# Attention and a ternary feed-forward on one core: VectorE takes y's rounding constant off while it clips, the ones are written by other memsets, and all five orders are new

## The chip, the cores and the metric

One NeuronCore of a Trainium2 chip runs the whole program. Its five engines (TensorE, VectorE, ScalarE, GpSimd, SyncE) follow instruction streams of their own and meet only at semaphores. The metric is the device time of one launch in microseconds. A profile calls the engines PE (PEld for weight loads), DVE, ACT, POOL and SP.

## The reference

32 batches of 128 channels by 512 positions (f32). Each batch goes through

```
x = x + attention(layernorm(x), ctx)     8 heads of 16 channels, rope on 8 of the 16,
                                         softmax over the 512 keys
x = x + ffn(layernorm(x))                gate, up: 512 -> 2048; silu(gate) * up;
                                         Hadamard transform over 2048; down: 2048 -> 512
act_quant(x):    q = 128 / max(max|x|, 1e-5);  clip(round(x q), -128, 127) / q
weight_quant(w): s = 1 / max(mean|w|, 1e-5);   clip(round(w s), -1, 1) / s
```

Every product with a weight of the feed-forward takes act_quant of its input (the down product that of the transformed y) and weight_quant of the weight.

## The kernel before, in words

One batch fills the 128 partitions. Its attention works in head chunks: 32 `score_max` products of 128 x 512 (L439), whose row maxima VectorE takes (`reduce_scores`, L1009); the maxima are transposed and laid by DMA into one more row of the stacked q, against a row of ones in the stacked k; 32 `scores` products (L469) then come out with the maximum taken off, ScalarE puts each through the exponential (`exps`, L712), and eight `weigh` groups (L484) multiply by v. `score_max` n may start when `reduce_scores` n - 2 is done, and `scores` n when `exps` n - 2 is done, since each has two PSUM banks.

The feed-forward of the batch before runs in the gaps: `gate_up` products (L525), `half_gates` (L1095), a tanh (L736), `glu` (L1104) and `gate_product` on GpSimd (L1274); then GpSimd makes four butterfly stages of the Hadamard transform: three on each half of 1024 columns (`hadamard_half`, L1265 the sums and L1266 the differences, with a semaphore wait after each stage), and the last over both (`hadamard_last`, L1263). TensorE multiplies by the 128 x 128 Hadamard matrix (`hadamard`, L536), ScalarE copies the four results into `ys` (`y_out`, L764), VectorE finds the largest value and the factor (`quantise`, L1116 to L1120).

Each half j of y (128 x 1024) is then quantised in three steps: ScalarE multiplies and adds the constant 12582912, which rounds (`round_y`, L743, f32); ScalarE takes the constant off again and writes bf16 (`whole_y`, L753); VectorE takes the minimum with 127 in place, bf16 to bf16 (`clip_y`, L1128). `y_transpose` j (L547) waits for that, `yT_out` (L771) copies it, and `down` (L560) multiplies.

The order of each engine is written out by hand in a function `step(t)`, called for t from `FIRST` to `LAST`; each call names the batch it serves (t, t - 1 and so on) and does nothing where that batch doesn't exist. All engines execute in this order. The three weights are loaded, their absolute means found (`abs_piece`), rounded (`round_piece`) and reduced to signs (`sign_piece`) in pieces between the work of the first three batches; the SP queue issues all activation DMAs in the order of its own `step`. GpSimd writes the row of ones of the first two stacks of k before its loop (L1233, one partition) and fills the third stack (L1240, all partitions) in the loop. `rstd1` (L1247) is the root of the first norm.

Of the kernel before, what the change touches and what calls it, by code (L numbers as in the profile page):

```python
# [39 lines left out]
FIRST, LAST = -3, B + 5  # L40


def live(b):
    return 0 <= b < B
# [45 lines left out]
def layer(nc, x, ctx_in, proj_t, table_t, late_t, wg_t, wu_t, wd_t, out):  # L90
    stack = ExitStack()
    with stack:
# [119 lines left out]
        ones_set, ones_rows_set, third_ones_set = sem("ones_set"), sem("ones_rows_set"), sem("third_ones_set")  # L212
# [15 lines left out]
        factor_done, rounded, whole = sem("factor_done"), sem("rounded"), sem("whole")  # L228
# [53 lines left out]
        def _(sp):  # L282
# [16 lines left out]
            def stack_part(b, part):  # L299
# [73 lines left out]
        def _(pe):  # L373
# [81 lines left out]
            def scores(b, n):  # L455
# [6 lines left out]
                if n == 0 and b == 0:  # L462
                    pe.wait_ge(ones_rows_set, 2)
                if n == 0 and b == 2:
                    pe.wait_ge(third_ones_set, 1)
# [98 lines left out]
            def step(t):  # L564
                gate_up(t - 3, "up", 3)
                scores(t - 2, 16)
                scores(t - 2, 17)
                score_max(t - 1, 16)
                score_max(t - 1, 17)
                weigh(t - 2, 3)  # L570
                scores(t - 2, 18)
                score_max(t - 1, 18)
                score_max(t - 1, 19)
                scores(t - 2, 19)
                scores(t - 2, 20)
                score_max(t - 1, 20)
                scores(t - 2, 21)
                down(t - 4, 0, 4)
                score_max(t - 1, 21)
                scores(t - 2, 22)  # L580
                scores(t - 2, 23)
                score_max(t - 1, 22)
                weigh(t - 2, 4)
                scores(t - 2, 24)
                scores(t - 2, 25)
                score_max(t - 1, 23)
                weigh(t - 2, 5)
                scores(t - 2, 26)
                score_max(t - 1, 24)
                scores(t - 2, 27)  # L590
                score_max(t - 1, 25)
                scores(t - 2, 28)
                score_max(t - 1, 26)
                scores(t - 2, 29)
                y_transpose(t - 4, 1)
                scores(t - 2, 30)
                score_max(t - 1, 27)
                score_max(t - 1, 28)
# [791 lines left out]
```

## Time and profile before

| | |
|---|---|
| three runs | 1533.31 us median, 1532.55 to 1535.38 |
| the profiled execution | 1531.52 us |
| its span, first to last instruction | 1529.7 us, mean granted clock of TensorE 0.974 |
| busy of the span | PE 93%, DVE 86%, ACT 71%, POOL 72%, PEld 49% |
| DMA | 71 GB/s mean |

The span falls into a start of some 170 us, in which weights and first batches are set up, 28 steady frames, one per batch, and an end of some 90 us in which the last feed-forwards run out. In a table of a stretch the five busy times are those of PE, PEld, DVE, ACT and POOL, in this order. A row of a timeline gives the start in us from the beginning of the span, the duration, engine, line, operation, destination and source. Neighbouring instructions overlap by some 0.08 us in it, so what one instruction costs an engine is the distance of two starts.

### The profile page before, as it was taken

To read this page: it belongs to the slowest core of one execution; us is meant where nothing else is said; L and a number is where in the kernel's file an instruction comes from. 1 tells how busy PE (TensorE), PEld (TensorE's weight loads), DVE (VectorE), ACT (ScalarE), POOL (GpSimd) and SP (SyncE) were. 2 spreads that over 40 slices of the span, in tenths; PEclk is the share of its full clock that TensorE was granted. 3 is DMA by queue.
4 is the path that set the end of the run, shared out by engine and by line. 5 is a ranking of instruction groups with operands and counts; after the bars stand their busy time and mean duration, and the time that the engine had idled before them with its cause. 6 is when DMAs were issued, how large, how long until landed. Compare 5 with 4: busy or idle time off the path is not lost.

```text
span 1529.7 us, 30990 instructions
## 1 busy us (share of the span) xinstructions
PE 1424.7 (93%) x11042; PEld 743.8 (49%) x11042; DVE 1322.4 (86%) x2331; ACT 1082.5 (71%) x1777; POOL 1098.7 (72%) x812
## 2 busy tenths in 40 slices
PE   1688999999999999999999999999999999999983
PEld 1215455545555555455555544555555444555442
DVE  2768899999999999999999999999999999998641
ACT  3586677778777777787777777877777777777762
POOL 4124777887777778877777788777777887777674
PEclk9688999999999999999999999999999999999996
DMA  8861434434234344343244443332434443323000
GB/s 211 223 124 37 66 63 77 70 63 69 61 60 77 63 77 76 58 70 63 58 76 63 77 77 61 66 65 61 70 64 77 77 68 59 69 46 47 15 8 14
DMA packets 81112, 108.12 MB, mean 71 GB/s; under 512 B 9664, under 2 KB 59200, under 8 KB 79936
## 3 DMA queue, kind: packets, MB, share of 16 engines
q1 hardware_dynamic: 77744, 93.56, 35.4%
q10 hardware_dynamic: 3216, 12.58, 2.3%
q8 instruction: 89, 1.46, 0.4%
q14 instruction: 63, 0.52, 0.1%
HBM read 38.73 MB, written 8.39 MB: 31 GB/s over the span
## 4 chain that ended last, share of the span: by engine, by line
PE 71%; ACT 12%; DVE 5%; issue 4%; POOL 4%; DMA 2%; SPq 0%; POOLq 0%; ACTq 0%; DVEq 0%
PE s L469 12%; PE ring L525 12%; PE pv L484 12%; PE s L439 11%; PE ring L560 7%; PE ring L536 6%; ACT region L712 4%; PE ring L413 3%; PE ring L493 2%; ACT parts L779 2%; PE ring L547 2%; PE ring L427 2%; ACT y_last L753 1%; ACT y_last L771 1%; DVE maxima L1009 1%
## 5 line engine op out<-in xcount | busy, mean ns | idle before, releaser
L1009 DVE TENSOR_REDUCE maxima<-s 128x1 bf16<-128x512 f32 x1024 | 668.3, 682 | 60.1 <-PE s L439 55.6
L712 ACT ACTIVATE region<-s 128x512 f32<-128x512 f32 x1024 | 576.0, 597 | 133.3 <-PE s L469 123.8
L439 PE MATMUL s<-region 96*128 96x512 bf16 x1024 | 374.3, 391 | 21.7 <-DVE maxima L1009 11.5
L1274 POOL TENSOR_TENSOR region<-region,th 128x512 f32<-128x512 f32 x128 | 161.8, 1273 | 297.1 <-DVE th L1104 295.3
L469 PE MATMUL s<-region 97*128 97x512 bf16 x1024 | 362.2, 384 | 10.0 <-ACT region L712 4.8
L1265 POOL TENSOR_TENSOR region<-region 128x512 f32<-128x512 f32 x192 | 260.3, 1356 | 12.8
L484 PE MATMUL pv<-region,v_ext 128*17 128x512 f32 x2048 | 264.1, 599 | 0.0
L1266 POOL TENSOR_TENSOR region<-region 128x512 f32<-128x512 f32 x192 | 243.9, 1270 | 0.0
L439 PEld LDWEIGHTS s<-region 96*128 96x128 bf16 x1024 | 99.8, 98 | 198.6 <-DVE maxima L1009 74.2
L469 PEld LDWEIGHTS s<-region 97*128 97x128 bf16 x1024 | 93.2, 98 | 187.7 <-ACT region L712 154.1
L1263 POOL TENSOR_TENSOR region<-region 128x1024 f32<-128x1024 f32 x64 | 149.4, 2355 | 0.1
L794 ACT ACTIVATE v_ext<-ring 128x512 f32<-128x512 f32 x32 | 19.1, 598 | 180.7 <-PE ring L427 178.2
L536 PE MATMUL ring<-late_const,region 128*128 128x128 f32 x1024 | 132.7, 279 | 13.7 <-POOL region L1263 11.7
L525 PEld LDWEIGHTS ring<-xqT,wg 128*128 128x128 bf16 x2048 | 123.5, 98 | 42.5 <-issue 16.7
L525 PEld LDWEIGHTS ring<-xqT,wu 128*128 128x128 bf16 x2048 | 122.4, 98 | 44.7 <-issue 26.6
L525 PE MATMUL ring<-xqT,wg 128*128 128x128 bf16 x2048 | 136.0, 219 | 7.4 <-ACT xqT L721 6.9
L536 PEld LDWEIGHTS ring<-late_const,region 128*128 128x128 f32 x1024 | 129.0, 195 | 18.0 <-issue 13.6
L525 PE MATMUL ring<-xqT,wu 128*128 128x128 bf16 x2048 | 135.7, 219 | 2.2 <-ACT y_last L771 1.2
L560 PE MATMUL ring<-wd,y_last 128*128 128x512 bf16 x512 | 127.6, 382 | 1.6 <-ACT y_last L771 1.6
L1095 DVE TENSOR_TENSOR region<-ring,half_gate 128x512 f32<-128x512 f32 x128 | 87.5, 684 | 13.5 <-PE ring L525 9.5
L1308 POOL TENSOR_TENSOR region<-region,rope_c 64x1024 f32<-64x1024 f32 x32 | 75.6, 2362 | 31.5 <-DVE region L998 17.4
L1104 DVE SCALAR_TENSOR_TENSOR th<-th,ring 128x512 f32<-128x512 f32 x128 | 87.3, 682 | 5.5 <-PE ring L525 4.2
(104 smaller groups left out, 1812.0 us busy)
## 6 DMA issues: line engine op xcount, KB each, us to landing
region<-parts SPq DMA_DIRECT2D x384, 128.0 KB, 4.8
x_in<-in_x SPq DMA_DIRECT2D x32, 256.0 KB, 2.6
c_in<-in_ctx SPq DMA_DIRECT2D x32, 256.0 KB, 2.9
rope_c<-region SPq DMA_DIRECT2D x64, 128.0 KB, 2.4
x_res<-in_x SPq DMA_DIRECT2D x32, 256.0 KB, 2.6
out<-o_sb SPq DMA_DIRECT2D x32, 256.0 KB, 2.4
region<-in_wg_t ACTq DMA_DIRECT2D x1, 2048.0 KB, 9.2
region<-in_wu_t ACTq DMA_DIRECT2D x1, 2048.0 KB, 7.3
```

The source lines that it names most:

```text
L439: pe.matmul(s1[p][:, :], q_stack[k][0:STACK, h, 128 * c:128 * (c + 1)], k_stack[k][0:STACK, h, :], start=True, stop=True).then_inc(s1_full ...
L469: pe.matmul(s2[n % 2][:, :], k_stack[k][0:STACK + 1, h, 128 * c:128 * (c + 1)], q_stack[k][0:STACK + 1, h, :], start=True, stop=True).then ...
L484: last = pe.matmul(pv[32 * i:32 * i + DH + 1, :], v_ext[b % 2][:, c, 4 * g + i, :], probs[:, (4 * u + i) % 8, :], start=(c == 0), stop=(c ...
L525: last = pe.matmul(bank(f"{name}{j}")[:, 128 * i:128 * (i + 1)], w[:, c, o:o + 128], xqT[:, c, :], start=(c == 0), stop=(c == HC - 1), ski ...
L536: last = pe.matmul(bank(f"y{j}")[:, 128 * c:128 * (c + 1)], z[:, o:o + 128], had[:, :], start=True, stop=True, skip_group_check=True)
L560: last = pe.matmul(bank("down")[:, :], yqT[:, c, :], wd[:, c, :], start=(c == 0), stop=(c == IC - 1))
L712: act.activation(probs[:, n % 8, :], s2[n % 2][:, :], ACT.Exp, scale=SCALE).then_inc(exp_done, 1)
L1009: dve.reduce_max(maxima[:, c, h:h + 1], s1[p][:, :], AXX).then_inc(s1_max[p], 1)
L1263: return pool.tensor_tensor(o[:, :, half, :], a[:, :, 0, :], a[:, :, 1, :], ALU.subtract if half else ALU.add)
L1265: pool.tensor_tensor(o[:, :, 0, :], a[:, :, 0, :], a[:, :, 1, :], ALU.add)
L1266: return pool.tensor_tensor(o[:, :, 1, :], a[:, :, 0, :], a[:, :, 1, :], ALU.subtract)
L1274: pool.tensor_tensor(zj, zj, th[:, j % 2, :], ALU.mult).then_inc(glu_done, 1)
```

## The change

`whole_y` is gone. `clip_y` reads the rounded f32 values and does minimum and subtraction in one instruction, f32 to bf16. The ones are written by one function for all three stacks, over all partitions, and the SP queue waits for them before the first part of a stack is laid. `FIRST` is -6, and the `step` of every engine but GpSimd is reordered; part of that is only another place to cut the loop.

```diff
-FIRST, LAST = -3, B + 5
+FIRST, LAST = -6, B + 5
@@ SyncE: stack_part, part 0
-                    if b == 2:
-                        sp.wait_ge(third_ones_set, 1)
+                    if b < 3:
+                        sp.wait_ge(ones_rows_set, b + 1)
@@ SyncE: step
-                load(t + 2)
-                stack_max(t - 1)
-                load_late_consts(t + 1)
+                stack_part(t + 1, 0)
                 load_residual(t - 1)
-                shift(t + 1)
-                store(t - 4)
                 load_consts(t + 3)
-                stack_part(t + 1, 0)
                 stack_part(t + 1, 1)
                 stack_part(t + 1, 2)
+                stack_max(t)
+                load(t + 3)
+                store(t - 3)
+                load_late_consts(t + 3)
+                shift(t + 2)
@@ ScalarE
-            def whole_y(b, j):
-                full(act, f"yT{j}", b - 1)
-                act.wait_ge(rounded, 2 * b + j + 1)
-                act.activation(yq[:, 1024 * j:1024 * (j + 1)], ys[:, 1024 * j:1024 * (j + 1)], ACT.Copy, bias=-ROUND) \
-                   .then_inc(whole, 1)
             def y_out(b, j):
-                wait(act, whole, 2 * (b - 1) + j // 2 + 1)
+                wait(act, yq_done, 2 * (b - 1) + j // 2 + 1)
@@ VectorE
             def clip_y(b, j):
-                dve.wait_ge(whole, 2 * b + j + 1)
-                half = yq[:, 1024 * j:1024 * (j + 1)]
-                dve.tensor_scalar(half, half, 127.0, None, ALU.min).then_inc(yq_done, 1)
+                full(dve, f"yT{j}", b - 1)
+                if b == 0:
+                    dve.wait_ge(ternary, UPTO[3])
+                dve.wait_ge(rounded, 2 * b + j + 1)
+                dve.tensor_scalar(yq[:, 1024 * j:1024 * (j + 1)], ys[:, 1024 * j:1024 * (j + 1)],
+                                  ROUND + 127, ROUND, ALU.min, ALU.subtract).then_inc(yq_done, 1)
@@ GpSimd
-            for k in range(2):
-                pool.memset(k_stack[k][STACK:STACK + 1, :, :], 1.0).then_inc(ones_rows_set, 1)
-                pool.wait_ge(ones_rows_set, k + 1)
-            def third_ones(b):
-                if b == 0:
-                    unstaged(pool, 2)
-                    pool.memset(k_stack[2][:, :, :], 1.0).then_inc(third_ones_set, 1)
+            def ones_rows(b, k):
+                if b == 0:
+                    unstaged(pool, k)
+                    pool.memset(k_stack[k][:, :, :], 1.0).then_inc(ones_rows_set, 1)
@@ GpSimd: step
+                ones_rows(t + 6, 0)
+                ones_rows(t + 6, 1)
                 rstd1(t + 1)
+                ones_rows(t - 1, 2)
                 gate_product(t - 2, 0)
-                third_ones(t - 1)
```

The order inside a steady frame, b being the batch whose `scores` run, differs in these places:

```
VectorE before: reduce 0, absmax, factors, reduce 1, quant_x, reduce 2, quantise, norm1_apply,
                half_gates 0, reduce 3, half_gates 1, glu 0, reduce 4, glu 1, reduce 5 ...
                ... half_gates 3, glu 2, reduce 14, 15, glu 3, 16 ... 19, 20, normalise 0, 21, clip_y 1, 22 ...
VectorE after:  reduce 0, absmax, factors, reduce 1, quant_x, reduce 2, reduce 3, quantise,
                half_gates 0, half_gates 1, reduce 4, glu 0, norm1_apply, glu 1, reduce 5 ...
                ... half_gates 3, reduce 14, glu 2, 15, glu 3, 16 ... 19, normalise 0, 20, clip_y 1, 21, 22 ...
TensorE before: scores 14, max 13, y_transpose 0, max 14, scores 15, weigh 2, max 15, up 3, scores 16, 17,
                max 16, 17, weigh 3, scores 18, max 18, 19, scores 19, 20, max 20, scores 21, down, max 21,
                scores 22, 23, max 22, weigh 4, scores 24, 25, max 23, weigh 5, scores 26, max 24, scores 27,
                max 25, scores 28, max 26, scores 29, y_transpose 1, scores 30, max 27, 28, scores 31,
                weigh 6, weigh 7, down, max 29, 30, down, max 31, attn_out, project_v, hadamard 0 ...
TensorE after:  max 13, scores 14, y_transpose 0, scores 15, max 14, weigh 2, scores 16, max 15, scores 17, up 3,
                scores 18, max 16, 17, scores 19, weigh 3, max 18, scores 20, max 19, scores 21, down, max 20,
                scores 22, 23, weigh 4, max 21, 22, scores 24, 25, weigh 5, scores 26, max 23, scores 27,
                max 24, scores 28, max 25, scores 29, max 26, y_transpose 1, scores 30, 31, max 27,
                weigh 6, max 28, weigh 7, down, max 29, 30, down, max 31, attn_out, project_v, hadamard 0 ...
ScalarE: gate_rows_out moves ahead of xqT_out; tanh 2 and tanh 3 stand behind exps 9 and exps 16,
         first_part behind exps 17, second_part behind exps 25
```

In the start, among others, both halves of w_down are loaded one after the other and ahead of the last `abs_piece` of w_up, the third `sign_piece` of w_up comes before the first `exps`, and `down_scale` moves behind the first `residual`.

## Rows read from the trace of the kernel before

**Rows 1.** Page, part 4: shares of the chain that ended last, by engine.

```profile
PE 71%; ACT 12%; DVE 5%; issue 4%; POOL 4%; DMA 2%; SPq 0%; POOLq 0%; ACTq 0%; DVEq 0%
```

**Rows 2.** A steady frame: busy us by engine (instructions), granted clock, DMA share, GB/s.

```profile
692.95:736.51 43.56, 43.11 (x347) 22.75 (x345) 40.85 (x73) 32.24 (x54) 33.96 (x26) 1.00 0.39 68
```

**Rows 3.** Timeline of VectorE in that frame: start, duration, instruction.

```profile
698.73 2.29 DVE L1116 TENSOR_REDUCE sc<-region 128x1 f32<-128x2048 f32 x1
...
701.75 0.54 DVE L980 TENSOR_SCALAR xn<-x_in,mv,rs 128x512 f32<-128x512 f32 x1
...
704.00 0.68 DVE L1104 SCALAR_TENSOR_TENSOR th<-th,ring 128x512 f32<-128x512 f32 x1
...
712.92 0.40 DVE L1128 TENSOR_SCALAR y_last<-y_last 128x1024 bf16<-128x1024 bf16 x1
...
723.47 1.96 DVE L1128 TENSOR_SCALAR y_last<-y_last 128x1024 bf16<-128x1024 bf16 x1
725.35 3.25 DVE L1009 TENSOR_REDUCE maxima<-s 128x1 bf16<-128x512 f32 x5
```

**Rows 4.** Timeline of GpSimd in that frame.

```profile
704.82 2.60 POOL L1274 TENSOR_TENSOR region<-region,th 128x512 f32<-128x512 f32 x2 [9.00 <-DVE th L1104]
...
712.65 1.81 POOL L1265 TENSOR_TENSOR region<-region 128x512 f32<-128x512 f32 x1
...
722.64 1.28 POOL L1265 TENSOR_TENSOR region<-region 128x512 f32<-128x512 f32 x1
723.87 1.28 POOL L1266 TENSOR_TENSOR region<-region 128x512 f32<-128x512 f32 x1
...
733.68 4.68 POOL L1263 TENSOR_TENSOR region<-region 128x1024 f32<-128x1024 f32 x2
```

**Rows 5.** Timeline of TensorE in that frame.

```profile
702.02 1.06 PE L525 MATMUL ring<-xqT,wg 128*128 128x128 bf16 x16
...
703.23 1.05 PE L484 MATMUL pv<-region,v_ext 128*17 128x512 f32 x8
...
714.54 0.61 PE L547 MATMUL ring<-eye_b,y_last 128*128 128x128 bf16 x8
...
720.23 0.85 PE L469 MATMUL s<-region 97*128 97x512 bf16 x2
...
727.47 0.39 PE L439 MATMUL s<-region 96*128 96x512 bf16 x1
...
729.33 1.91 PE L484 MATMUL pv<-region,v_ext 128*17 128x512 f32 x16
```

**Rows 6.** Groups of VectorE by line and shape: busy us, mean ns, idle before.

```profile
L1081 DVE TENSOR_SCALAR xq<-turned_pv 128x512 bf16<-128x512 f32 x32 | 13.4, 418 | 1.1 <-ACT turned_pv L810 0.9
...
L962 DVE TENSOR_SCALAR region<-region,w_inv 128x2048 f32<-128x2048 f32 x7 | 8.8, 1281 | 0.0
...
L962 DVE TENSOR_SCALAR region<-region,w_inv 128x1024 f32<-128x1024 f32 x6 | 4.3, 746 | 0.0
```

**Rows 7.** Timeline of the start: memsets, first and second root, VectorE's rounding beside the second.

```profile
1.27 7.07 POOL L1233 MEMSET region<- 1x4096 bf16 x2
...
7.90 0.15 DVE L973 TENSOR_SCALAR ve<-mv 128x1 f32<-128x1 f32 x1
8.43 0.56 POOL L1247 TENSOR_TENSOR rs<-ve,half_neg 128x1 f32<-128x1 f32 x1
...
34.63 3.68 DVE L962 TENSOR_SCALAR region<-region,w_inv 128x2048 f32<-128x2048 f32 x3
34.78 2.37 POOL L1247 TENSOR_TENSOR rs<-ve,half_neg 128x1 f32<-128x1 f32 x1 [5.12 <-DVE ve L973]
```

**Rows 8.** The chain that ended last: first row of maxima, and a `whole_y` near the end.

```profile
76.29 6.08 DMA region<-neg_max
...
1445.33 0.83 ACT y_last L753
```

**Rows 9.** Timeline of ScalarE in the last batch.

```profile
1516.63 1.06 ACT L753 ACTIVATE y_last<-region 128x1024 bf16<-128x1024 f32 x1
```

More of the change, by code:

```diff
@@ L821, in step @@
             def step(t):
-                load_weights(t + 3, 0, 0)
+                abs_piece(t - 2, 2, 2)
+                exps(t - 2, 15)
+                abs_piece(t, 0, 0)
+                exps(t - 2, 16)
+                abs_piece(t, 0, 1)
+                tanh(t - 3, 3)
+                exps(t - 2, 17)
+                abs_piece(t - 1, 1, 0)
+                first_part(t)
+                exps(t - 2, 18)
+                exps(t - 2, 19)
+                exps(t - 2, 20)
+                exps(t - 2, 21)
@@ L870, in step @@
                 tanh(t - 2, 0)
                 exps(t - 1, 5)
+                tanh(t - 2, 1)
+                load_weights(t + 2, 0, 0)
                 sign_piece(t - 2, 2, 3)
-                tanh(t - 2, 1)
+                round_y(t - 3, 0)
+                abs_piece(t - 1, 2, 0)
+                sign_piece(t, 0, 2)
                 sign_piece(t - 2, 2, 4)
-                round_y(t - 3, 0)
+                abs_piece(t - 1, 2, 1)
                 sign_piece(t - 2, 2, 5)
                 exps(t - 1, 6)
-                whole_y(t - 3, 0)
@@ L1139, in step @@
             def step(t):
+                reduce_scores(t - 1, 16)
+                reduce_scores(t - 1, 17)
+                reduce_scores(t - 1, 18)
+                reduce_scores(t - 1, 19)
+                normalise(t - 2, 0)
+                reduce_scores(t - 1, 20)
+                clip_y(t - 4, 1)
+                reduce_scores(t - 1, 21)
+                reduce_scores(t - 1, 22)
+                reduce_scores(t - 1, 23)
+                reduce_scores(t - 1, 24)
+                round_piece(t, 0, 0)
@@ new lines, in step @@
+                round_piece(t, 0, 1)
+                reduce_scores(t - 1, 25)
+                reduce_scores(t - 1, 26)
+                norm1_stats(t + 1)
+                reduce_scores(t - 1, 27)
+                late_consts(t)
+                reduce_scores(t - 1, 28)
+                normalise(t - 2, 1)
+                reduce_scores(t - 1, 29)
+                reduce_scores(t - 1, 30)
+                up_scale(t - 1)
+                turn_back(t - 2)
+                final(t - 4)
+                round_piece(t, 0, 2)
@@ new lines, in step @@
+                gate_factors(t - 2)
+                reduce_scores(t, 1)
+                quant_x(t - 2)
+                reduce_scores(t, 2)
+                round_piece(t - 2, 2, 4)
+                round_piece(t - 2, 2, 5)
+                reduce_scores(t, 3)
+                quantise(t - 3)
+                round_piece(t - 2, 2, 6)
+                half_gates(t - 2, 0)
+                half_gates(t - 2, 1)
+                reduce_scores(t, 4)
+                glu(t - 2, 0)
+                norm1_apply(t + 1)
@@ new lines, in step @@
+                glu(t - 2, 1)
+                reduce_scores(t, 5)
+                reduce_scores(t, 6)
+                round_piece(t - 1, 1, 3)
+                half_gates(t - 2, 2)
+                rope_sin(t + 1, 0)
+                reduce_scores(t, 7)
+                rope_sin(t + 1, 1)
+                round_piece(t, 0, 3)
+                reduce_scores(t, 8)
+                round_piece(t - 2, 2, 7)
+                reduce_scores(t, 9)
+                rope_cos(t + 1, 0)
+                reduce_scores(t, 10)
```

236 lines of the change are left out of this document (79 added, 157 removed).

## The prediction

> **What bounds the kernel now.** I read the page's chain first: TensorE has 71% of it, ScalarE 12%, the rest is small [rows 1]. A mean over the span hides where a frame is tight, so I took one steady frame, from the first Hadamard product of a batch to that of the next, 43.56 us. In it TensorE is busy 43.11, VectorE 40.85, GpSimd 33.96, ScalarE 32.24 us, at the full granted clock [rows 2]. Two readings follow. ScalarE has 11 us of air, so work taken from it pays only where its queue is late. VectorE has 2.7 us, so work given to it is nearly on the path.
>
> Then I walked through the frame engine by engine. TensorE hardly stops. Two `scores` took 0.85 us at 720.23, behind a `whole_y` that had held ScalarE's exponentials; with their neighbours I put this loss at 0.4 us. Before the product of 727.47, which waits for VectorE or an exponential, another 0.3 us are lost [rows 5]. Those 0.7 us are an estimate of all that the change can win in a frame on these two waits.
>
> GpSimd is not the bound but close to it. It starts at 704.82, when the first `glu` is done, and works without a hole until both last butterflies are done; the first of them ends near 736.03 and its consumer starts at 736.51 [rows 2, 4]. Less 0.1 for the semaphore, the slack is 0.37 us. Whatever makes that `glu` later, or stretches GpSimd, counts from 0.37 us on.
>
> The third thing is the clip. The same instruction takes 0.40 us at 712.92 and 1.96 us at 723.47 [rows 3]; I found this pair in 27 of the 28 steady frames, at the same places. At 712.92 GpSimd's sum takes 1.81 instead of 1.28 us [rows 4]: it waits for VectorE. At 723.47 VectorE waits: the sum and the difference run back to back to 725.15, and the clip ends at 725.43, 0.28 later. So they exclude each other, and VectorE gets in only at the wait between two butterfly stages. The five reductions behind it start at 725.35, and TensorE's product of 727.47 is near the last of them in time [rows 3, 5]. This stretch is where the frame will be decided.
>
> **The parts.** 1. *`whole_y` goes.* 64 times 1.06 us of ScalarE, less the overlap of 0.08 [rows 9]. In a steady frame ScalarE's other work hides it except the 0.4 us at 720.
>
> 2. *The clip from f32.* 128x1024 f32 to bf16 isn't in the trace. Below: the same pair of operations on 512 columns, 0.418 us. Above: 0.746 us for 128x1024 f32 to f32 with a per-partition factor. The slope between 1024 and 2048 columns is 0.535 us, so 512 more columns on the first row give 0.418 + 0.267 = 0.69 us; I take that [rows 6]. Against 0.40 it is 0.29 us more, 0.58 per frame, on VectorE and on what it shares with GpSimd.
>
> Does the f32 form exclude GpSimd as the bf16 form does? The root of the norm, 0.56 us at 8.43, took 2.37 us at 34.78, beside three f32 roundings of VectorE that began at 34.63 [rows 7]. It does. The Trainium skill (SBUF — State Buffer, "Who interferes with whom") says that a `tensor_scalar` in a two-port mode and a GpSimd instruction hold the shared ports for a whole instruction, and that the one issued first blocks the other. The rows agree, with one addition: of two GpSimd instructions without a wait between them VectorE gets nothing, as at 723.87. By the rule alone a clip could also get in there, and the second clip would end 1.3 us earlier, which is rival B.
>
> 3. *VectorE's order ahead of the first `glu`.* Reduction 3 now stands before `quantise`: 698.73 becomes 699.33. `quantise` keeps its 3.02 us (698.73 to 701.75): `half_gates` 0 at 702.35. `half_gates` 1 would follow at 702.95, but its product ends at 702.02 + 1.06 = 703.08 [rows 5], so 703.15; reduction 4, then `glu` 0 at 704.35 instead of 704.00 [rows 3]. GpSimd starts at 705.17: 0.35 us later. That eats the 0.37 us of slack and moves everything of GpSimd in the frame.
>
> 4. *The first clip.* Same instructions ahead of it, so again near 712.95, while GpSimd's stage wait moves to 712.9 to 713.0. It gets in, takes 0.69, and delays the sum by about as much as before. `y_transpose` 0 at 714.54 [rows 5] isn't touched. Nothing either way.
>
> 5. *The second clip.* Ahead of it VectorE has 16 to 19, `normalise`, 20. `glu` 3 now waits for an `up` 3 that stands behind `scores` 16, 17 and `score_max` 15, so this comes to 723.3. GpSimd's pair runs from 722.98 to 725.49. The clip then waits, and ends at 725.49 + 0.28 + 0.29 = 726.06, 0.63 later than before. And reduction 21, done before the clip until now, stands behind it. `score_max` 26 needs reduction 24: four reductions, 0.60 from start to start (0.68 less the overlap), from 725.98, done at 728.46, product at 728.53 instead of 727.47: 1.06 us.
>
> 6. *TensorE's order behind it.* `score_max` 28 parts `weigh` 6 from 7. 16 products in one row take 1.91 us, 8 take 1.05, and by my estimate one change between the kinds costs some 0.1 [rows 5]. Against it `y_transpose` 1 and the rest stand as before: 0.05 to 0.2 us more, I take 0.05. The wait at 720 goes, but with `score_max` 26 waiting for VectorE this gives nothing. So a frame is 1.1 us longer: 44.7. GpSimd, 0.35 and perhaps 0.3 late, is then off the path.
>
> 28 frames: +30.8 us.
>
> 7. *The start.* The title says that the memsets now stand behind the first root. They don't: `ones_rows(t + 6, k)` fires at t = -6, `rstd1(t + 1)` at t = -1. Two memsets over 4096 columns took 7.07 us on one partition and held the root from 8.05 to 8.43 [rows 7]; over 128 partitions the third, one of the same length, took as long, so this is 0. Were they behind, it would be -0.4. The SP queue issues the first row of maxima ahead of the next batch's loads; it took 6.08 us [rows 8] beside w_down's load, of which more will now be under way: between -3.5 and +2, I take -1. A `sign_piece` leaves the first batch's exponentials: -1. Together -2 us (-5 to +2). The other reordered pieces, and SP's stores, residuals and shifts, move inside waits of several us.
>
> 8. *The end.* In the last batch nothing lies beside the y chain: a `whole_y` of 1.06 and a clip of 0.40 become one clip of 0.69: -0.77 [rows 3, 9]. In the last attention ScalarE is on the chain, with 0.83 us of one `whole_y` [rows 8] and part of another: -1.2. Together -2.
>
> Sum: 30.8 - 2 - 2 = +26.8. The profiled execution took 1531.5, so 1558.3; the median of the runs is 1.8 above it: **1560 us**.
>
> **Rivals.** A is the forecast: with 0.8 to 1.4 us a frame 1552 to 1569 us.
>
> B, *the second clip costs less than I think*: it gets the ports at once or after one instruction, or the reductions behind it have air. Then TensorE isn't held, and the frame goes to GpSimd's loop: 43.56 - 0.37 + 0.35 = 43.54. Nothing in the frames, -4 and -0.5 at the ends: 1529. If also the 0.35 isn't there, up to 0.4 a frame more: 1517. For it: ScalarE is 2 us lighter in each frame, and the planned places fit a clip of 0.7 us without a wait. Against it: the 1.96 us in 27 frames.
>
> C, *GpSimd becomes the bound*: the clip gets in ahead of the pair, ends early, and holds GpSimd 0.5 us. Loop: 43.54 + 0.5 = 44.04, +0.48 a frame, +13.4 - 4: 1543. It decides once the clips stretch GpSimd by over 0.02 us more than before, and only if A's wait doesn't come first.
>
> D, *the first clip misses the gap*: VectorE comes 0.2 us too late, waits for a pair (2.5 us), and `y_transpose` 0 starts at 716.2 instead of 714.6: +1.6 a frame, which covers A's: +45 - 4: 1574.
>
> E, *nothing to see*: half of A's wait in part of the frames, or B without its gain at the ends: within 0.2%, 3 us, which is what a measurement here can tell from no change.
>
> **How the numbers follow.** A 0.42, B 0.27, C 0.13, D 0.08, E 0.10. Slower is A, C and D: 0.63; same 0.10; faster 0.27. The range takes in A, C, E and nearly all of B, and stops at D: 1516 to 1574.
>
> **What would show it.** Right: the second clip 2.6 us or longer in the steady frames, with reduction 21 behind it and the products of `score_max` 23 to 26 released by VectorE 0.6 us apart; a frame of 44.7; GpSimd's first `gate_product` 12.2 us after the frame's first Hadamard product instead of 11.87; the first root still right behind two memsets of 3.5 us. Wrong: clips of 0.7 at both places; a frame of 43.6 or less; the Hadamard products waiting for L1263 (C); `y_transpose` 0 waiting for VectorE (D).

## The result, and the profile after

The changed kernel takes 1559.57 us (median of 4 runs, 1556.69 to 1559.89) against 1534.35 us of the kernel before in the same comparison: a ratio of 1.016 with an interval of 1.014 to 1.0179. It is slower, by 1.6%. 1560 was predicted. The profiled execution took 1559.86 us, its span is 1558.1 us. The two profiled executions are 28.3 us apart and the medians 25.2, since that of the kernel before (1531.52) lies under its median.

The first thing to read is the page: busy time by engine, then the shares of the chain that ended last.

```profile
PE 1424.1 (91%) x10980; PEld 738.3 (47%) x11042; DVE 1353.7 (87%) x2331; ACT 1018.4 (65%) x1713; POOL 1108.2 (71%) x812
...
PE 67%; DVE 16%; issue 5%; ACT 4%; POOL 4%; DMA 3%; SPq 1%; ACTq 0%; POOLq 0%; DVEq 0%
```

ScalarE lost 64 us of work and two thirds of its share of the chain, VectorE went from 5 to 16% [rows 1]. TensorE does the same work in more time. That GpSimd has only 4% is the trap of this case, as will be seen.

Then the frame, from one batch's first Hadamard product to the next. Columns as in [rows 2]:

```profile
796.37:840.87 44.50, 43.37 (x345) 22.52 (x346) 41.84 (x73) 30.30 (x52) 34.29 (x26) 1.00 0.38 67
```

It lasts 44.50 us instead of 43.56. There are 28 steady frames; the 27 intervals between their first clips add up to 1201.50 us, against 1177.03: +24.5 us. The first of these clips stands at 193.62 instead of 189.44 (+4.2), and from the last of these clips to the end of the span it is 162.98 instead of 163.23 (-0.3). The sum, 28.4, is the difference of the two profiled executions.

VectorE in this frame (start, duration, instruction): `glu` 0, `norm1_apply` and `glu` 1, the two clips, the reductions behind the second. They answer to [rows 3].

```profile
807.84 0.68 DVE L1087 SCALAR_TENSOR_TENSOR th<-th,ring 128x512 f32<-128x512 f32 x1
808.43 0.54 DVE L963 TENSOR_SCALAR xn<-x_in,mv,rs 128x512 f32<-128x512 f32 x1
808.89 0.68 DVE L1087 SCALAR_TENSOR_TENSOR th<-th,ring 128x512 f32<-128x512 f32 x1
...
816.47 0.68 DVE L1113 TENSOR_SCALAR y_last<-region 128x1024 bf16<-128x1024 f32 x1
...
826.64 2.90 DVE L1113 TENSOR_SCALAR y_last<-region 128x1024 bf16<-128x1024 f32 x1
829.45 3.67 DVE L992 TENSOR_REDUCE maxima<-s 128x1 bf16<-128x512 f32 x6
```

GpSimd in the same stretch [rows 4]. The two sums of 1.71 and 1.60 are those that a clip made longer; undisturbed, one takes 1.26 to 1.28.

```profile
808.66 2.67 POOL L1256 TENSOR_TENSOR region<-region,th 128x512 f32<-128x512 f32 x2 [9.66 <-DVE th L1087]
...
816.57 1.71 POOL L1247 TENSOR_TENSOR region<-region 128x512 f32<-128x512 f32 x1
...
826.49 1.26 POOL L1247 TENSOR_TENSOR region<-region 128x512 f32<-128x512 f32 x1
827.71 1.27 POOL L1248 TENSOR_TENSOR region<-region 128x512 f32<-128x512 f32 x1
829.06 1.60 POOL L1247 TENSOR_TENSOR region<-region 128x512 f32<-128x512 f32 x1
...
837.22 0.62 POOL L1280 TENSOR_TENSOR mixed<-turned_pv,inv_sum 128x256 f32<-128x256 f32 x1
```

TensorE behind the second clip [rows 5]: `score_max` products released by VectorE; the next ones follow at 830.79, 831.39 and 831.99, 0.60 apart.

```profile
830.19 0.39 PE L439 MATMUL s<-region 96*128 96x512 bf16 x1 [0.61 <-DVE maxima L992]
...
833.41 1.05 PE L480 MATMUL pv<-region,v_ext 128*17 128x512 f32 x8
834.71 1.05 PE L480 MATMUL pv<-region,v_ext 128*17 128x512 f32 x8
```

So far this is what the prediction described. But a wait that is there, where it was expected and as long as expected, need not be what sets the frame. The runs show that what this wait does through VectorE is a quarter of the loss.

**A loop of two parts.** Take GpSimd's timeline and note two instructions per frame: the first `gate_product` (L1274 before, L1256 after) and the second product of `mix` (L1298 before, L1280 after). Between them GpSimd works without a hole; from the second `mix` the way leads over `attn` on VectorE, the output projection, norm 2, the quantisation of x, the gate and up products and `glu` 0 back to the next `gate_product`. In the kernel before, GpSimd and then VectorE:

```profile
791.94 2.60 POOL L1274 TENSOR_TENSOR region<-region,th 128x512 f32<-128x512 f32 x2 [9.00 <-DVE th L1104]
...
820.22 0.62 POOL L1298 TENSOR_TENSOR mixed<-turned_pv,inv_sum 128x256 f32<-128x256 f32 x1
```

```profile
819.58 1.29 DVE L1009 TENSOR_REDUCE maxima<-s 128x1 bf16<-128x512 f32 x2 [0.15 <-PE s L439]
820.94 0.71 DVE L1029 STREAM_TRANSPOSE attn<-mixed 128x512 f32<-128x512 f32 x1
```

`attn` starts 0.72 us after the second `mix` does (0.62 of work and 0.1), while the reduction ahead of it ends at 820.87: VectorE and GpSimd arrive there together. It is 28.28 us from product to `mix` and 15.27 us from `mix` to product (the next is at 835.49). That the two add up to the frame proves nothing, since both ends are the same instruction of neighbouring frames. What shows a loop without slack is that GpSimd doesn't stop in the first part, that the second part comes out at 15.27 in five kernels below whose first parts range from 28.28 to 28.99 and where `attn` follows `mix` by 0.72, and that the edits of the experiments change one part and the frame follows. This is the link that I missed. The same two numbers for twelve kernels of this study, each from one frame near 800 us of its profile; the medians over the steady frames differ from them by 0.05 at most (the kernel of experiment 6 has those of the changed kernel, and in that of experiment 8 GpSimd does stop):

| kernel | product to second mix | second mix to product | frame | first clip after its sum's start | median us |
|---|---|---|---|---|---|
| before | 28.28 | 15.27 | 43.55 | 0.26 | 1534.35 |
| after | 28.56 | 15.94 | 44.50 | -0.10 | 1559.57 |
| f32 clip, old orders | 28.80 | 15.27 | 44.07 | 0.26 | 1546.97 |
| new orders, old clip | 28.37 | 15.87 | 44.24 | -0.10 | 1556.11 |
| after, clip 1 behind 21 | 28.50 | 15.70 | 44.20 | -0.10 | 1555.66 |
| after, clip 1 behind 22 | 28.56 | 15.70 | 44.26 | -0.11 | 1554.12 |
| after, old glu order | 28.97 | 15.52 | 44.49 | 0.38 | 1561.01 |
| after, three edits | 28.99 | 15.27 | 44.26 | 0.39 | 1550.70 |
| after, old glu order, clip 0 earlier | 28.50 | 15.27 | 43.77 | -0.19 | 1543.17 |
| before, clip 0 earlier | 27.81 | 15.57 | 43.38 | -0.33 | 1528.64 |
| before, both clips placed | 27.81 | 15.57 | 43.38 | -0.33 | 1527.86 |
| the same with f32 clips | 28.33 | 15.27 | 43.60 | -0.34 | 1534.23 |

The loss of 0.95 us a frame is then 0.28 in GpSimd's part and 0.67 in the way back: 0.43 for the glu order and 0.24 for the second clip's wait, which makes `attn` late. The experiments take these two out.

The 0.28 is not the clips alone. The sums beside the clips give 0.17 (1.71 for 1.80, and 1.60 for 1.34). Another 0.08 lies between the first two `gate_product`s, whose starts are 1.41 apart instead of 1.33: in the new order `norm1_apply`, a `tensor_scalar` too, stands between `glu` 0 and `glu` 1, and the first product beside it takes 1.45 us, where the kernel before has 1.27:

```profile
808.66 1.45 POOL L1256 TENSOR_TENSOR region<-region,th 128x512 f32<-128x512 f32 x1 [9.66 <-DVE th L1087]
```

The old glu order brings the 1.27 back (experiments 5, 7 and 9), so that order costs 0.43 + 0.08. Those 0.17 and 0.08 are medians over the frames, and 0.03 are the scatter of the one frame of the table.

### The profile page after: what moved, and what is told of

The parts are those of the page before. It is cut to its first block, busy times and chain, and to the rows that moved or that the text cites. A ratio compares the mean times of both kernels' runs of the same rounds, so it can differ in the third digit from the quotient of the medians.

```text
span 1558.1 us, 30865 instructions
## 1 busy us (share of the span) xinstructions
PE 1424.1 (91%) x10980; PEld 738.3 (47%) x11042; DVE 1353.7 (87%) x2331; ACT 1018.4 (65%) x1713; POOL 1108.2 (71%) x812
## 4 chain that ended last, share of the span: by engine, by line
PE 67%; DVE 16%; issue 5%; ACT 4%; POOL 4%; DMA 3%; SPq 1%; ACTq 0%; POOLq 0%; DVEq 0%
PE ring L521 15%; PE s L439 12%; PE pv L480 12%; PE s L465 10%; DVE maxima L992 6%; DVE y_last L1113 5%; PE ring L556 5%; PE ring L413 4%; PE ring L532 3%; PE ring L489 2%; PE ring L427 2%; PE ring L543 2%; DMA region<-parts 2%; DVE turned_pv L1002 1%; ACT xqT L717 1%
## 5 line engine op out<-in xcount | busy, mean ns | idle before, releaser
L708 ACT ACTIVATE region<-s 128x512 f32<-128x512 f32 x1024 | 568.6, 594 | 222.4 <-PE s L465 217.0
L439 PE MATMUL s<-region 96*128 96x512 bf16 x1024 | 380.7, 392 | 48.1 <-DVE maxima L992 35.6
L1256 POOL TENSOR_TENSOR region<-region,th 128x512 f32<-128x512 f32 x128 | 165.1, 1308 | 316.2 <-DVE th L1087 316.0
L1247 POOL TENSOR_TENSOR region<-region 128x512 f32<-128x512 f32 x192 | 266.7, 1389 | 13.1 <-ACT wd L697 0.3
L480 PE MATMUL pv<-region,v_ext 128*17 128x512 f32 x2048 | 270.1, 600 | 0.2 <-DVE turned_pv L1002 0.2
L1248 POOL TENSOR_TENSOR region<-region 128x512 f32<-128x512 f32 x192 | 245.2, 1277 | 0.0
L465 PEld LDWEIGHTS s<-region 97*128 97x128 bf16 x1024 | 96.5, 98 | 137.9 <-ACT region L708 70.3
L556 PE MATMUL ring<-wd,y_last 128*128 128x512 bf16 x450 | 113.6, 382 | 8.5 <-issue 4.8
L1113 DVE TENSOR_SCALAR y_last<-region 128x1024 bf16<-128x1024 f32 x64 | 109.8, 1715 | 1.6 <-ACT region L739 1.6
```

The lines of the kernel that those rows point to most:

```text
L439: pe.matmul(s1[p][:, :], q_stack[k][0:STACK, h, 128 * c:128 * (c + 1)], k_stack[k][0:STACK, h, :], start=True, stop=True).then_inc(s1_full ...
L465: pe.matmul(s2[n % 2][:, :], k_stack[k][0:STACK + 1, h, 128 * c:128 * (c + 1)], q_stack[k][0:STACK + 1, h, :], start=True, stop=True).then ...
L480: last = pe.matmul(pv[32 * i:32 * i + DH + 1, :], v_ext[b % 2][:, c, 4 * g + i, :], probs[:, (4 * u + i) % 8, :], start=(c == 0), stop=(c ...
L556: last = pe.matmul(bank("down")[:, :], yqT[:, c, :], wd[:, c, :], start=(c == 0), stop=(c == IC - 1))
L708: act.activation(probs[:, n % 8, :], s2[n % 2][:, :], ACT.Exp, scale=SCALE).then_inc(exp_done, 1)
L1113: dve.tensor_scalar(yq[:, 1024 * j:1024 * (j + 1)], ys[:, 1024 * j:1024 * (j + 1)], ROUND + 127, ROUND, ALU.min, ALU.subtract).then_inc(yq ...
```

## The experiments

Medians of the kernel before in their comparisons were 1533.36 to 1534.07 us.

**1. The clip alone: old orders, f32 clip, no `whole_y`.** Compared with the kernel before (cut, with `half` short for the 1024 columns of half j; the waits change as in the change itself):

```
-                whole_y(t - 3, 0)
-                whole_y(t - 3, 1)
...
-                dve.tensor_scalar(half, half, 127.0, None, ALU.min)
+                dve.tensor_scalar(yq[half], ys[half], ROUND + 127, ROUND, ALU.min, ALU.subtract)
```

> The kernel before with the new clip alone: whole_y gone, clip_y from f32 in one instruction, all orders and memsets as before. Port theory (the second clip waits for GpSimd's sum and difference, then VectorE's reductions behind it release TensorE's products): the clip asks at the same place, gets in at the same wait of GpSimd, and holds on 0.28 us longer; a steady frame goes from 43.56 to about 43.8, and with about 1.5 us won at the ends the time is near 1534 + 7 - 2 = 1539 us. Clips 0.68 and 2.25 us. Rival, relief of ScalarE: the 1.9 us a frame taken from ScalarE end the wait at the exponentials, the frame falls to 43.2, the time to about 1523 us; the 25 us of the change then come from the orders alone.

Measured: 1546.97 us, ratio 1.0089 (1.0072 to 1.0105), frame 44.07: 8 us over the expected time. The second clip takes 2.48 us, 0.52 more than before, and yet the way back is 15.27, as before: that wait costs nothing here. The whole 0.52 is in GpSimd's part: the sum beside the first clip takes 2.07 instead of 1.80, the one behind the second 1.60 instead of 1.34.

**2. The orders alone: new orders, `whole_y` and the bf16 clip back.** The reverse of the edit above, on the changed kernel.

> The changed kernel with the old quantisation in three steps (whole_y on ScalarE, bf16 clip on VectorE), each whole_y behind the exponential it stood behind before; orders, memsets and step limits as changed. Port theory: the second clip ends 0.28 us earlier, still at GpSimd's wait, and reduction 21 still stands behind it: frame 44.2 instead of 44.5, time near 1560 - 8 + 2 = 1554 us. Clips 0.40 and 2.6 us. Rival, the f32 clip is the whole cost: the frame is back at 43.6 and the time near 1537 us.

Measured: 1556.11 us, ratio 1.0145 (1.0129 to 1.016), frame 44.24. The second clip takes only 0.89 us, not the 2.6 expected: it gets in between a sum of GpSimd and its difference, in all 28 steady frames. The frame is still 0.69 longer. It is the way back that grew, by 0.60: 0.42 is the glu order (experiment 5), and 0.19 that `attn` starts 0.91 after `mix` and not 0.72. This sank the account that the second clip's long wait sets the frame. VectorE's clip, then GpSimd:

```profile
825.25 0.89 DVE L1124 TENSOR_SCALAR y_last<-y_last 128x1024 bf16<-128x1024 bf16 x1
```

```profile
821.26 1.28 POOL L1266 TENSOR_TENSOR region<-region,th 128x512 f32<-128x512 f32 x1 [0.21 <-DVE th L1100]
...
824.58 1.28 POOL L1257 TENSOR_TENSOR region<-region 128x512 f32<-128x512 f32 x1
825.81 1.47 POOL L1258 TENSOR_TENSOR region<-region 128x512 f32<-128x512 f32 x1
```

GpSimd's part, 28.37, is no measure of the orders alone: the first row is a stop of about 0.2 us that the other kernels of the table don't have in most frames. The `glu` that it waits for had waited 0.98 us for a tanh of ScalarE, which here has `whole_y` to do besides. So in the new orders taking `whole_y` off ScalarE seems to be worth those 0.2 us; no run shows it by itself.

**3 and 4. The changed kernel with the second clip behind reduction 21, or behind 22.**

```
                 reduce_scores(t - 1, 20)
-                clip_y(t - 4, 1)
                 reduce_scores(t - 1, 21)
                 reduce_scores(t - 1, 22)
+                clip_y(t - 4, 1)
```

> The changed kernel with reduction 21 ahead of the second clip, one swap in VectorE's order. Port theory: the clip still ends at the same place, but TensorE's score_max 23 to 26 are released one reduction (0.60 us) earlier; the frame is 43.9, the time 1560 - 16 = 1544 us, and the clip 2.35 us. If GpSimd's loop sets a floor (slack read as 0.63 us in the changed kernel), it is just touched. Rival, the whole length of the clip counts and not what stands behind it: no change, 1560 us.

> The changed kernel with the second clip behind reductions 21 and 22, so that it asks shortly before GpSimd's wait comes. Port theory: the clip waits 0.5 us instead of 2.27, about 1.2 us long in all, and VectorE no longer holds TensorE. With GpSimd's loop as the next bound the frame is 43.9 (44.5 less the 0.6 us of slack that it shows now), the Hadamard product waits for L1245, and the time is 1560 - 16 = 1544 us. Without such a bound the frame would be 43.2 and the time 1525 us. Rival, GpSimd and VectorE don't exclude each other and the clip is long of itself: it still takes 2.9 us, now later, and the frame is 44.5 or longer.

Measured: behind 21, clip 1.52 us, 1555.66 us, ratio 1.0145 (1.0128 to 1.0162); behind 22, clip 0.93 us, 1554.12 us, 1.0132 (1.0116 to 1.0148). Of the 2.27 us of wait 1.4 and 2.0 were taken away and the frame fell by 0.24 to 0.30, not by the 0.6 expected; both times are 10 us or more over the expected 1544. Here VectorE's timeline names the new releaser, behind 22:

```profile
834.10 1.29 DVE L992 TENSOR_REDUCE maxima<-s 128x1 bf16<-128x512 f32 x2 [0.15 <-PE s L439]
835.58 0.71 DVE L1012 STREAM_TRANSPOSE attn<-mixed 128x512 f32<-128x512 f32 x1 [0.19 <-POOL mixed L1280]
```

`attn` now waits for GpSimd. In the changed kernel it started 0.98 us after the second `mix` (838.20 and 837.22), here 0.73 (835.58 and 834.85). The rest of the loss is in GpSimd's part and in the glu order. The Hadamard product, which I had expected to wait for GpSimd, doesn't.

**5. The changed kernel with the old glu order.**

```
-                reduce_scores(t, 3)
                 quantise(t - 3)
+                norm1_apply(t + 1)
                 half_gates(t - 2, 0)
+                reduce_scores(t, 3)
                 half_gates(t - 2, 1)
-                reduce_scores(t, 4)
                 glu(t - 2, 0)
-                norm1_apply(t + 1)
+                reduce_scores(t, 4)
```

> The changed kernel with one piece of VectorE's order as before: quantise, norm1_apply, half_gates 0, reduction 3, half_gates 1, glu 0, reduction 4, glu 1. Theory G (GpSimd's loop sets the frame): from GpSimd's first gate_product to its second mix, then through attn, wo, the Hadamard products, quantise and glu 0 back to gate_product, 28.56 + 15.94 = 44.50 us in the changed kernel against 28.28 + 15.27 = 43.55 in the kernel before. The old glu order gives back 0.43 of the second part: frame 44.07 (43.83 if the late attn of 0.24 goes with it), time 1559.6 - 28 x 0.43 = 1547.5 us. Theory A (my prediction: the second clip's wait sets the frame and GpSimd's later start is off the path): frame 44.50, 1560 us.

Measured: 1561.01 us, ratio 1.0178 (1.0161 to 1.0195), frame 44.49: no gain, so the expected time was wrong by 13.5 us. The way back did fall by 0.42, to 15.52. But GpSimd's part rose by 0.41, to 28.97: the first `gate_product` gave back 0.08 and the sum beside the first clip took 0.49 more. Its timeline, and VectorE's, at the first clip:

```profile
817.75 2.20 POOL L1247 TENSOR_TENSOR region<-region 128x512 f32<-128x512 f32 x1
```

```profile
818.13 0.68 DVE L1113 TENSOR_SCALAR y_last<-region 128x1024 bf16<-128x1024 f32 x1
```

GpSimd arrives 0.4 us earlier and VectorE doesn't, so the same clip now comes 0.38 us after the recorded start of the sum, and still has the ports first: the sum takes 2.20. In all twelve kernels of the table the sum beside the first clip is longer than 1.27 by the same expression, the clip's end less the sum's start less 0.13 to 0.14: 0.53 before (800.04 + 0.41 - 799.78), 0.44 after, 0.93 here and in experiment 7, down to 0.07 in experiment 10. The `gate_product` beside `norm1_apply` fits it too (808.43 + 0.54 - 808.66 less 0.13 is 0.18, and it takes 1.45 for 1.27). By the durations, then, GpSimd begins its work some 0.14 before the recorded end of the VectorE instruction, whatever its own recorded start says. What the clip costs is decided by where it stands against the sum, to a tenth of a microsecond.

**6. The start: the second half of `w_down` at its old place.**

```
                 abs_piece(t, 0, 2)
-                load_weights(t - 1, 2, 1)
...
+                load_weights(t - 1, 2, 1)
                 gate_rows_out(t - 2)
                 xqT_out(t - 2)
```

> The changed kernel with the second half of w_down loaded where the kernel before loads it, after the first batch's y pieces and ahead of xqT, instead of right behind the first half. Theory: the two halves side by side on the DMA queues hold batch 1's stack parts (17.29 us for one at 67.11) and so score_max(1, 0), which TensorE meets ahead of scores(0, 0); with them apart, score_max(1, 0) stands near 80 instead of 84.45 and the first clip near 189.5 instead of 193.62: 4 us less, 1555.5 us; frames unchanged at 44.50. Rival: the start is later by the new orders on SP and ScalarE themselves: within 1 us of 1559.6.

Measured: 1558.74 us, ratio 1.0165 (1.015 to 1.018): no difference that can be told from the changed kernel. TensorE's wait for a stack part is shorter, as expected. First the changed kernel, then this one:

```profile
84.45 1.03 PE L439 MATMUL s<-region 96*128 96x512 bf16 x2 [7.77 <-DMA region<-parts]
```

```profile
80.95 1.03 PE L439 MATMUL s<-region 96*128 96x512 bf16 x2 [4.76 <-DMA region<-parts]
```

So the two loads side by side do hold batch 1's stack. But of the 3.5 us there are 2.1 left at GpSimd's first `gate_product` (139.29 and 141.36) and 0.5 at the first clip (193.08 and 193.62). The other 3.7 us of the start stay open, and one pair of executions can't settle them. The two kernels of experiment 10 have the same orders up to their first clip, and a rounding of VectorE ahead of it stands at 154.31 in one and at 151.69 in the other. Over all traces GpSimd's first `gate_product` stands at 136.1 to 140.6 in the six kernels with the old orders in the start, at 140.8 to 142.1 in the six with the new orders and the halves of `w_down` together, and at 139.3 and 138.4 in the two with them apart (this one and experiment 7). TensorE's wait is 7.7 to 8.1 us in each of those six, and 4.8 and 4.7 in these two. So the two loads may well be some 2 us of the later start, and the kernel before had the earliest start of its six; the time of this run alone shows neither.

**7. The changed kernel with three edits:** the old glu order, the second clip behind 22, `w_down` apart.

> The changed kernel with three edits: the glu order of before, the second clip behind reductions 21 and 22, and w_down's second half at its old place. Theory G: GpSimd's part 28.56 plus 15.27, frame 43.83; 1559.6 - 28 x 0.67 - 4 = 1537 us. What is left against the kernel before is then the clips' theft of GpSimd's ports, 0.28 us a frame. Theory A: with the wait of the clip gone the frame is back to 43.56: 1529.6 us. If neither loop but the order of TensorE's products sets 44.2: 1551 us.

Measured: 1550.70 us, ratio 1.0114 (1.0099 to 1.0129), frame 44.26. Way back 15.27, the old value to the hundredth, so the two terms of 0.43 and 0.24 are all there is in it. Theory G's time was missed all the same, by 14 us: GpSimd's part is 28.99 and not 28.56, with the first clip at 0.39 after the sum's start, as in 5. The number that fits is that of the third theory, 1551 us, by which the order of TensorE's products sets 44.2. This run can't tell it from the loop; experiment 9 can, since it has the same new order of TensorE and a frame of 43.77.

**8. The kernel before, first clip later.** The clip behind `rope_cos` 1 and reductions 12 and 13, with `y_transpose` 0 and `yT_out` 0 moved to match (those two moves are not shown).

```
-                clip_y(t - 2, 0)
                 rope_cos(t + 2, 1)
                 reduce_scores(t + 1, 12)
                 reduce_scores(t + 1, 13)
+                clip_y(t - 2, 0)
```

> The kernel BEFORE (whole_y and bf16 clip kept) with only the first clip moved behind rope_cos 1 and reductions 12 and 13, y_transpose 0 behind weigh 2, and yT_out 0 behind tanh 3. The clip then should come while a pair of GpSimd runs, wait for its end and take the ports at the stage wait, which lengthens GpSimd's next instruction by 0.07 instead of 0.53 us. Theory G: GpSimd's part falls from 28.28 to 27.82; its loop to 43.1, then TensorE, busy 43.11 in a frame, is the bound with some stops: frame 43.35 (43.2 to 43.5), 1534.35 - 28 x 0.2 = 1528.5 us, which would beat the kernel before. Rival: TensorE and VectorE set 43.56 by themselves: no gain, 1534 or more, since VectorE loses 0.4 us here.

Measured: 1669.60 us, ratio 1.0882 (1.0863 to 1.0901), where 1528.5 was expected; frames mostly of 46.8 to 49.8, 48.2 in the mean. GpSimd, then VectorE:

```profile
819.93 1.27 POOL L1266 TENSOR_TENSOR region<-region 128x512 f32<-128x512 f32 x1
821.28 2.34 POOL L1308 TENSOR_TENSOR region<-region,rope_c 64x1024 f32<-64x1024 f32 x1
825.24 1.26 POOL L1274 TENSOR_TENSOR region<-region,th 128x512 f32<-128x512 f32 x1 [1.62 <-DVE th L1104]
```

```profile
821.38 2.52 DVE L1128 TENSOR_SCALAR y_last<-y_last 128x1024 bf16<-128x1024 bf16 x1
```

The reduction ahead of the clip waited 0.48 us for TensorE, the clip came 0.1 us after GpSimd's `turn` had begun, and waited for its end: 2.52 us for 0.40 of work. `half_gates` 3 and `glu` 2 and 3 behind it came late and GpSimd, which must never stop, stopped for 1.6 us twice. That is rival D's mechanism, at two to four times its price of 1.6 us a frame. The moves of `y_transpose` 0 and `yT_out` 0 weren't tried apart from it.

**9. The first clip earlier, in the changed kernel with the old glu order.**

```
                 reduce_scores(t, 10)
+                clip_y(t - 3, 0)
                 reduce_scores(t, 11)
-                clip_y(t - 3, 0)
```

> The changed kernel with the old glu order (as in the run glu order back, frame 44.49) and the first clip one reduction earlier in VectorE's order, ahead of reduction 11. There the clip started 0.38 us after GpSimd's sum and still had the ports first, and stretched the sum to 2.20 us (1.27 plus 0.93; clip end less sum start less about 0.13). 0.6 us earlier it comes while GpSimd's pair still runs, is let in at the stage wait and stretches the sum by 0.34 only. Theory G: GpSimd's part 28.97 - 0.59 = 28.38, plus 15.52, frame 43.90; 1561.0 - 28 x 0.59 = 1544.5 us. If the second clip, 0.59 us late against GpSimd then, misses its place, up to 0.6 of it is lost again. Theory A (the second clip's wait holds TensorE): frame 44.5, 1561.

Measured: 1543.17 us, ratio 1.0059 (1.0042 to 1.0075), frame 43.77: 17.8 us less than in experiment 5, by one line. The sum beside the first clip takes 1.61. The second clip found the place that it had in experiment 2 and that the prediction had held impossible. VectorE, then GpSimd:

```profile
819.51 1.15 DVE L1113 TENSOR_SCALAR y_last<-region 128x1024 bf16<-128x1024 f32 x1
```

```profile
818.83 1.27 POOL L1247 TENSOR_TENSOR region<-region 128x512 f32<-128x512 f32 x1
820.07 1.73 POOL L1248 TENSOR_TENSOR region<-region 128x512 f32<-128x512 f32 x1
```

It got in between a sum and its difference, which have no wait between them. Since `attn` is no longer late, the way back is 15.27 here and not the 15.52 expected.

**10. The same one-line move in the kernel before** (reduction 11 behind the clip), **and with the second clip behind reduction 22 too.**

> The kernel BEFORE with one edit: the first clip stands ahead of reduction 11 instead of behind it, 0.6 us earlier (799.44 instead of 800.04 in the frame at 791.94). GpSimd's pair ends at 799.70; the clip waits for that, ends at about 799.99, and the sum behind it takes 1.34 instead of 1.80. Theory G: GpSimd's part 28.28 - 0.46 = 27.82, its loop 43.09; then TensorE, busy 43.11 in a frame, is the bound with some stops: frame 43.3 (43.15 to 43.5), 1534.35 - 28 x 0.26 = 1527 us, ratio 0.995. Rival: TensorE and VectorE set 43.56 by themselves: 1534, ratio 1.000.

> The kernel BEFORE with the first clip ahead of reduction 11 and the second behind reduction 22. The second clip waits 1.55 us of its 1.96 at 810.59; with GpSimd 0.46 earlier its pair ends at 811.3, and a clip that comes at 811.2 gets the ports at once, so VectorE wins about 1 us and the reductions that TensorE waits for at 814.4 come earlier. Theory G: as the run with the first clip alone, then 0.1 a frame less: 43.2, 1524 us. Against it: if the clip comes after 811.3 it either holds GpSimd's next sum (up to 0.8 us) or waits for a whole pair (2.5 us, with a frame of 44 to 46 and up to 1600 us).

Measured: 1528.64 us, ratio 0.9965 (0.9951 to 0.9978), and 1527.86 us, 0.9965 (0.9953 to 0.9977). Both are faster than either kernel of the case, by 0.35% against the kernel before. The first clip, and the sum beside it, in the first of the two:

```profile
801.48 0.54 DVE L1128 TENSOR_SCALAR y_last<-y_last 128x1024 bf16<-128x1024 bf16 x1
```

```profile
801.81 1.34 POOL L1265 TENSOR_TENSOR region<-region 128x512 f32<-128x512 f32 x1
```

GpSimd's part fell to 27.81, the 27.82 expected. The loop would then take 43.08, but the way back is 0.30 longer: `attn` starts 1.04 after the second `mix` (822.83 and 821.79), behind two reductions that start at 821.62, after TensorE's `score_max` products of 821.20. So GpSimd has slack at last. TensorE, busy 42.82 of 43.38 us, is what I take for the bound now, but its idle 0.56 us a frame are no less than the 0.45 of before, and no run tried it:

```profile
771.29:814.67 43.38, 42.82 (x346) 22.73 (x344) 40.36 (x74) 32.23 (x56) 33.48 (x26) 1.00 0.39 68
```

The second clip, 0.89 instead of 1.49 us in the second kernel, changes nothing in the frame (43.38 in both), where I had given it 0.1.

**11. The same places with f32 clips and without `whole_y`.**

> The kernel BEFORE with the change's clip (from f32, no whole_y) and with the places of the run both clips placed: the first clip ahead of reduction 11, the second behind reduction 22. Theory G: each f32 clip of 0.68, let in at a stage wait, stretches GpSimd's sum by 0.34, two of them by 0.68, where those of the kernel before stretch by 0.53 + 0.07: GpSimd's part 28.28 + 0.08 = 28.36, plus 15.27: frame 43.63, 0.25 above the same places with bf16 clips (43.38). 1534 + 28 x 0.07 = 1536, less 1.6 at the ends, as in the run with the f32 clip in the old orders: 1534.5 us, ratio 1.000. Rival: ScalarE, lighter by two whole_y, lets TensorE run at its own bound: 43.38 or less, 1526 us, ratio 0.995. If a clip misses its place: 44.0 or more, over 1545 us.

Measured: 1534.23 us, ratio 1.0004 (0.9995 to 1.0013), frame 43.60. This is the change's idea in the best places found: it removes two `whole_y` a frame from ScalarE, which isn't in the loop, and lengthens two sums of GpSimd, which is. 28.33 and 15.27 are the loop's numbers again, 28.36 and 15.27 the expected ones. The relief of ScalarE, the rival, gives nothing here.

## Why the prediction was right, and where it wasn't

*Frame: +1.1 predicted, +0.94 measured.* The time is right, its reason only in part. The prediction's step that failed is in its first part: GpSimd's slack "is 0.37 us", read where the first Hadamard product follows the last butterfly [rows 4], and its consequence in step 6, that GpSimd is "then off the path". GpSimd has a second consumer 3 us earlier, `attn`, with no slack. I had stopped at the last instruction of GpSimd instead of going through all that wait for it.

*Step 2, the clip's duration and ports:* 0.68 for 0.69. The exclusion is there. The Trainium skill (SBUF — State Buffer, "Who interferes with whom") has the shared ports held for a whole instruction by whoever was issued first. The 2.52 us clip and the 2.20 us sum agree; its "first" isn't the order of the recorded starts, since 0.38 us after the sum's start the clip was still first. The clips of 1.96 and 2.95 us go beyond that rule: they waited for two instructions of GpSimd, and for only one in experiments 2 and 9.

*Step 3, `glu` 0:* +0.35 predicted, +0.42 from the first Hadamard product (11.47 and 11.05), 0.43 in the way back. Right, and it counts in full, where the prediction let the slack eat it. That `norm1_apply`, moved behind `glu` 0, holds GpSimd's first product for another 0.08 was not in it.

*Step 4, the first clip, "nothing either way":* roughly so in the changed kernel, by luck. It came 0.36 us earlier against the sum than before and is 0.27 longer, so the sum takes 1.71 and not 1.80.

*Step 5, the second clip:* 2.7 us predicted, 2.94 to 2.97 in 26 of 28 frames (2.78 and 2.90 in the others); reduction 21 behind it and TensorE's products 0.60 apart, as predicted. But +1.06 was charged and 0.24 is its share (experiments 3 and 4); its stretch of GpSimd's sum, 0.33 instead of 0.07, costs about as much, and wasn't charged.

*Step 6, TensorE's order:* `weigh` 6 and 7 are two rows of 1.05 instead of one of 1.91. With TensorE off the path no run could show a price.

*Rivals.* C, GpSimd as the bound, had the mechanism in part and 0.13 of the chances. Its price of 0.48 a frame took 0.35 for `glu` 0, but set the 0.37 of slack against it, gave the clips 0.5 where they cost 0.17, and had nothing for the late `attn` (0.24). B's condition, a second clip that hardly waits, was met behind 22 (0.25 us of wait) and nearly in experiment 2 (0.48): 1554 and 1556 us and not 1529. The prediction's argument against B, that VectorE gets nothing between two GpSimd instructions without a wait, was wrong, and its own trace had the counterexample in the one frame that it left out: at 320.76 the first clip waited for a sum only, took 0.97 us and lengthened the difference to 1.45.

*Step 7, the start:* -2 predicted, +4.2 measured. The memsets stand ahead of the root as predicted:

```profile
1.28 6.96 POOL L1222 MEMSET region<- 128x4096 bf16 x2
8.29 0.56 POOL L1229 TENSOR_TENSOR rs<-ve,half_neg 128x1 f32<-128x1 f32 x1
```

*Step 8, the end:* -2 predicted, -0.3 measured. The last batch's clips take 0.69 each in place of 1.06 and 0.40; where the other microsecond went wasn't tried.

The whole came out at 1560 by luck. In the frame the missing terms (0.28 and 0.43) and the term charged too high (1.06 for 0.24) nearly cancel. What is left of it, 30.8 us for the frames where 24.5 were measured between the first clips, is made up by the start and end, -4 where +3.9 was measured.

## What to carry to other kernels

Look for the loop, not for the busiest engine: an engine at 78% of the frame that never pauses between two points, with a fixed way back from the second to the first, sets the period, and the chain that ended last still gave it 4%. Measure slack at every consumer of such an engine, and follow the two parts of the loop through an edit: their sum is the frame in any case, but which of them moves is what an experiment tells. Then go through the gap-free part instruction by instruction, since here three of them (two sums and a product) were stretched by three different instructions of VectorE. An instruction that shares ports with such an engine belongs where it waits for the engine's own pause; here starts of 0.2 to 0.5 us ahead of GpSimd's next instruction cost it least. One line moved by one reduction was worth 5 us in one kernel and 18 in another, and moved the other way, past three instructions and with what depends on it, it cost 136.

## What the hardware showed that I had not expected

The clip's claim on the ports reaches back before its recorded start: GpSimd instructions that began up to 0.39 us earlier by their own record still waited for it, and by their durations began their work 0.14 us before the clip's recorded end, in twelve kernels. In the one kernel where the reduction just ahead of the first clip had itself waited for TensorE (experiment 8, 0.48 us), the clip had no such claim: it lost to an instruction 0.10 us ahead. Whether that wait is the reason wasn't tried.

Two GpSimd instructions without a wait between them are no closed door either: in all 28 steady frames of experiments 2 and 9 the second clip came mostly 0.67 us into the sum and got in ahead of the difference (1.47 and 1.73 instead of 1.27 us), while in the changed kernel, 0.15 us into the sum, it waited for both. The offset alone doesn't decide: in experiment 1 the clip waited for both at 0.56, in the kernel before at 0.83, and in twelve frames of experiment 8 it got in at offsets from 0.2 to 0.9. What decides wasn't found.
